# Residual and bias row accumulated in the output's PSUM bank of a sequence mixer, and gathers of the expert choice issued six experts ahead

## The chip, the cores and the metric

The kernel runs on one core of one Trainium2 chip, as a single launch. The metric is the device time of that launch in microseconds (us), the median of several runs. Differences of about 0.3% are what the measurement can tell from no change.

## What is computed

The reference is two transformer blocks over `x[16, 512, 128]` in fp32: causal attention with ALiBi slopes, an expert-choice feed-forward layer (8 experts, each takes the 256 tokens with its highest router score), a gated convolution and state-space mixer, and a top-2-of-8 mixture of experts. The change touches the second and the third. The expert choice, with `xf` the normalised tokens:

```python
G, idx = jax.lax.top_k(softmax(xf @ router_w + router_b).T, K)      # K = 256 tokens for each of 8 experts
toks = xf[idx]
h1 = relu(einsum('ekh,ehf->ekf', toks, w1) + b1[:, None, :])
eo = einsum('ekf,efh->ekh', h1, w2) + b2[:, None, :]
y = zeros_like(xf).at[idx.reshape(-1)].add((eo * G[..., None]).reshape(-1, h))
```

The mixer, with `x` here the layer-normalised input (the caller adds the outer residual):

```python
u, v = split(x @ in_proj_w + in_proj_b)
v_local = dwconv(silu(v), conv_w, conv_b)                # 3 taps along time
h_t = a * h_{t-1} + ssm_b * v_local_t;  y_t = ssm_c * h_t + ssm_d * v_local_t
out = (u * silu(y)) @ out_proj_w + out_proj_b
h = out + x
return (h - mean(h)) * rsqrt(var(h) + 1e-5) * ln_w + ln_b
```

## The kernel before

The kernel runs its stages one after the other, each in a block of its own that ends with all engines meeting: attention, projection, choice of tokens, `expert_choice`, `mixer`, gate and dispatch, `experts`.

**expert_choice.** For each of the 8 experts GpSimd (POOL) issues two gathers of 128 rows by indirect DMA into `xg` (L1142). TensorE turns them (`turn`, L1191), computes router logits, the first matrix (`first`, L1204) and the second (`second`, L1216); ScalarE applies the relu, VectorE the gates and the product with the score into `ctr` (L1288). POOL then adds the two tiles of `ctr` to `x_scr` by two indirect DMAs with an add (the scatters, L1157). A scatter waits until `ctr` of its expert is there (`s_ctr`) and until every earlier scatter has landed (`s_sc`), because two experts can add to one row. POOL's order is written out: gathers of experts 0 to 2; then for each expert e the gathers of e+3 followed by the scatters of e. Weights are loaded by SyncE in two buffers each.

**mixer.** Sixteen sequences of 512 positions. The loop is software-pipelined (`skewed`): in step s each engine works on block s (normalise, turn, input projections), block s-1 (convolution, recurrence, gate) and block s-2 (output projection, residual, second norm). Buffers alternate by the parity of the block. The order of the work on each engine in a step is:

- TensorE (PE): output projection of s-2 into `psO` (L1428, 4 products), turn of s into `psX` (L1435), `psV` (L1440), `psU` (L1443).
- ScalarE (ACT): `xn` of s (L1463, 4 tiles), copy `xT` (L1468), `dv` of s-1, `vs` (L1477) and `c0` (L1479) of s, `ys` of s-1 (L1485), `hn` of s-2 (L1493, 4 tiles).
- VectorE (DVE): tap 0 of s-1 (L1550), `ho` = `psO` + `xo` of s-2 (L1560), tap 2 of s-1 (L1550), 4 `bn_stats` of `ho` (L1566), the seven small instructions of `chain` (L1512 to L1522) that end in `veps`, scan of s-1 (L1579), `y` (L1582), 4 `bn_stats` of s+2 (L1504), `z` of s-1 (L1592).
- POOL: `rstd` (a power, L1384) and `shift` (L1386) from `veps`, `t2` (L1402), `xo` = `xn` + bias row (L1407), `t1` (L1410), a short instruction (L1413), the final sum into `x_all` (L1414).

`chain` serves x of block s+1 and h of block s-2 at once, so `shift` releases `hn` of s-2 and then `xn` of s+1.

Of the kernel before, what the change touches and what calls it, by code (L numbers as in the profile page):

```python
# [13 lines left out]
F32 = mybir.dt.float32  # L14
# [8 lines left out]
P = 128  # L23
# [1078 lines left out]
def expert_choice(nc, idx, tab, rw, rb, w1, b1, w2, b2, xbuf, ident, nb):  # L1102

    nt = nb * TT
    FT = 4
    SCORE = 6
    with ExitStack() as ctx:
        sb = lambda name, shape, dt: ctx.enter_context(nc.sbuf_tensor("ec_" + name, shape, dt))
# [30 lines left out]
        def _(pool):  # L1139
# [4 lines left out]

            for e in range(3):
                gather(e)
            for e in range(E):
                if e + 3 < E:
                    pool.wait_ge(s_xg[e % 3], 32 * (e // 3 + 1))
                    gather(e + 3)  # L1150

                pool.wait_ge(s_ctr, e + 1)
                if e:
                    pool.wait_ge(s_sc, 32 * e)
                for k in (2 * e, 2 * e + 1):
                    off = bass.IndirectOffsetOnAxis(ap=idx[:, k:k + 1], axis=0)
                    pool.indirect_dma_start(xr, off, ctr[:, k, :], None, compute_op=ALU.add).then_inc(s_sc, 16)  # L1157
# [155 lines left out]
def mixer(nc, x_all, xbuf, ident, win, wout, prm, rows, loads, nb):  # L1313

    with ExitStack() as ctx:
# [18 lines left out]
            "a", "b", "c", "minus_mean", "var", "veps", "rstd", "shift"))  # L1334
        xn, xT, vs, c0, vl, hs, dv, ys, z, xo, ho, hn = (two(n, s) for n, s in (
            ("xn", [P, TT, C]), ("xT", [P, T]), ("vs", [P, T + 2]), ("c0", [P, T]), ("vl", [P, T]), ("hs", [P, T]),
            ("dv", [P, T]), ("ys", [P, T]), ("z", [P, T]), ("xo", [P, TT, C]), ("ho", [P, TT, C]), ("hn", [P, TT, C])))
        t1, t2 = sb("t1", [P, TT, C], F32), sb("t2", [P, TT, C], F32)
# [4 lines left out]
        psO = [ps("psO0"), ps("psO1")]  # L1343
        s_w, s_p, s_set, s_xs, s_hs, s_n, s_r, s_xn, s_tr, s_xT, s_uv, s_vs, s_c0, s_c, s_dv, s_y, s_ys, s_z, s_o, s_xo, \
            s_h, s_hn, s_t1, s_x3, s_pre, s_v, s_ahead = (sem(n) for n in (
                "weights", "powers", "set", "x_stats", "h_stats", "chain", "shift", "xn_ready", "turned", "xT_ready", "uv_ready",
                "v_ready", "conv0", "conv", "dv_ready", "y_ready", "silu_y", "z_ready", "out_ready", "xo_ready", "h_ready",
                "hn_ready", "t1_ready", "x3_ready", "prepared", "v_product", "loaded_ahead"))
# [25 lines left out]
        def _(pool):  # L1374
# [15 lines left out]
            def step(s, n):  # L1390
# [10 lines left out]
                if live(b, nb):  # L1401
                    pool.tensor_tensor(t2[:], x_all[:, bass.ds(TT * b, TT), :], rows_s[:, 2], ALU.add)  # L1402
                if live(s, nb):
                    pool.wait_ge(s_xn, s + 1)
                    if not isinstance(s, int) or s >= 2:
                        pool.wait_ge(s_h, s - 1)
                    pool.tensor_tensor(xo[n][:], xn[n][:], rows_s[:, 0], ALU.add).then_inc(s_xo, 1)  # L1407
                if live(b, nb):
# [9 lines left out]
        def _(pe):  # L1418
            pe.wait_ge(s_w, 16 * (TT + 3))

            def step(s, n):
                b = s - 2
                if live(b, nb):
                    pe.wait_ge(s_z, b + 1)
                    if not isinstance(b, int) or b >= 2:
                        pe.wait_ge(s_h, b - 1)
                    for t in range(TT):
                        i = pe.matmul(psO[n][:, P * t:P * t + P], z[n][:, P * t:P * t + P], wout_s[:], start=True, stop=True)  # L1428
                    i.then_inc(s_o, 1)
                if live(s, nb):  # L1430
                    pe.wait_ge(s_xn, s + 1)
# [15 lines left out]
        def _(act):  # L1447
# [7 lines left out]
            def step(s, n):  # L1455
                m = 1 - n
                if live(s, nb):
                    act.wait_ge(s_r, s + 1)
                    if not isinstance(s, int) or s >= 2:
                        act.wait_ge(s_tr, s - 1)  # L1460
                        act.wait_ge(s_xo, s - 1)
                    for t in range(TT):
# [23 lines left out]
                if live(s - 2, nb):  # L1486
# [4 lines left out]
                    for t in range(TT):  # L1491
                        u = TT + t
                        i = act.activation(hn[n][:, t], ho[n][:, t], ACT.Identity, bias=shift[:, u:u + 1], scale=rstd[:, u:u + 1])  # L1493
                    i.then_inc(s_hn, 1)
# [3 lines left out]
        def _(dve):  # L1498
# [36 lines left out]
            dve.wait_ge(s_pre, 4)  # L1535

            def step(s, n):
                m = 1 - n
# [715 lines left out]
```

## Time and profile before

| | us |
|---|---|
| median of 3 runs | 1726.03 (1721.57 to 1727.01) |
| the profiled execution | 1718.55 |
| its span, first to last instruction | 1716.7 |
| expert choice, from the first gather to the last scatter | 875.4 to 948.0 |
| mixer, from its first instruction to its last | 950.3 to 1130.5 |

The span has a tensor clock of 0.836 of full speed on average. The mixer's steady steps lie between 980 and 1126 us. Rows of the timeline give start and duration of one instruction (or of equal neighbours, with their count), and in brackets how long the engine was idle before it and what ended that.

### The profile page before, as it was taken

To read this page: it belongs to the slowest core of one execution; us is meant where nothing else is said; L and a number is where in the kernel's file an instruction comes from. 1 tells how busy PE (TensorE), PEld (TensorE's weight loads), DVE (VectorE), ACT (ScalarE), POOL (GpSimd) and SP (SyncE) were. 2 spreads that over 40 slices of the span, in tenths; PEclk is the share of its full clock that TensorE was granted. 3 is DMA by queue.
4 is the path that set the end of the run, shared out by engine and by line. 5 is a ranking of instruction groups with operands and counts; after the bars stand their busy time and mean duration, and the time that the engine had idled before them with its cause. 6 is when DMAs were issued, how large, how long until landed. Compare 5 with 4: busy or idle time off the path is not lost. (4 is left out here: it accounts for less than half of the span.)

```text
span 1716.7 us, 35014 instructions
## 1 busy us (share of the span) xinstructions
PE 1226.1 (71%) x9530; PEld 728.2 (42%) x9531; DVE 1164.2 (68%) x3272; ACT 837.4 (49%) x2073; POOL 990.9 (58%) x1023
## 2 busy tenths in 40 slices
PE   2788788888777888584046366627099999999997
PEld 1334333433333433373035133327066655555555
DVE  2778687777666778386732499866866666666664
ACT  1567576766666677111212366634144444444443
POOL 1465455655454553241035399965268888888887
PEclk7899899999989999565568655655599999999999
DMA  4433333433322431362023200300423333333333
GB/s 112 144 82 92 73 105 90 96 88 93 77 71 77 95 96 62 116 222 73 0 85 73 68 26 25 118 6 24 181 38 41 42 42 43 41 41 42 41 43 40
DMA packets 88430, 125.49 MB, mean 73 GB/s; under 512 B 22434, under 2 KB 59106, under 8 KB 84242
## 3 DMA queue, kind: packets, MB, share of 16 engines
q0 software_dynamic: 41120, 45.22, 16.7%
q1 hardware_dynamic: 39170, 65.85, 11.5%
q10 hardware_dynamic: 8032, 12.93, 2.1%
q8 instruction: 74, 1.21, 0.3%
q14 instruction: 34, 0.28, 0.1%
HBM read 65.72 MB, written 57.68 MB: 72 GB/s over the span
## 5 line engine op out<-in xcount | busy, mean ns | idle before, releaser
L548 DVE TENSOR_REDUCE mx<-psS 128x2 f32<-128x768 f32 (+3 forms) x384 | 386.3, 1041 | 169.7 <-PE psS L441 169.0
L619 ACT ACTIVATE probs<-psE 128x512 f32<-128x512 f32 (+2 forms) x768 | 345.2, 523 | 162.4 <-PE psE L455 160.3
L344 POOL TENSOR_SCALAR_AFFINE_SELECT probs<-probs 128x512 f32<-128x512 f32 x256 | 162.1, 642 | 261.2 <-ACT probs L619 260.9
L2034 POOL DMA_INDIRECT out<-ex_y,ex_idx x144 | 236.7, 1644 | 47.5 <-issue 43.0
L455 PE MATMUL psE<-qop,kop 63*128 63x512 bf16 (+3 forms) x1024 | 195.5, 312 | 78.9 <-DVE rest L514 34.8
L467 PE MATMUL psY<-probs,vaug 128*32 128x512 f32 (+3 forms) x2048 | 180.8, 464 | 9.7 <-POOL probs L344 9.7
L2025 POOL DMA_INDIRECT ex_xg<-expert_tab,ex_idx x144 | 141.9, 985 | 66.0 <-issue 41.7
L2008 DVE SCALAR_TENSOR_TENSOR ex_h<-ex_psG,ex_w,ex_up 128x352 f32<-128x352 f32 x144 | 84.0, 584 | 106.1 <-PE ex_psG L2075 95.4
L441 PE MATMUL psS<-kop,qop 61*128 61x128 bf16 (+3 forms) x1024 | 141.8, 310 | 0.0
L2092 PE MATMUL ex_psY<-ah_w3s,ex_hT 128*128 (+1 forms) x864 | 133.2, 290 | 0.9 <-ACT ex_hT L2103 0.7
L455 PEld LDWEIGHTS psE<-qop,kop 63*128 63x128 bf16 x1024 | 65.1, 96 | 160.2 <-ACT probs L619 91.5
L436 PE MATMUL psS<-maskq,spread 64*128 64x128 bf16 (+2 forms) x1536 | 115.2, 227 | 19.9 <-DVE mx L548 19.8
L2102 ACT ACTIVATE ex_hT<-ex_psH 128x256 f32<-128x256 f32 x144 | 55.2, 383 | 135.5 <-PE ex_psH L2068 127.3
L2092 PEld LDWEIGHTS ex_psY<-ah_w3s,ex_hT 128*128 128x128 f32 (+1 forms) x864 | 107.6, 191 | 21.1 <-issue 3.5
L2074 PE MATMUL ex_psU<-ah_w1s,ex_xT 128*128 x288 | 110.1, 464 | 0.5 <-ACT ex_xT L2113 0.5
L436 PEld LDWEIGHTS psS<-maskq,spread 64*128 64x128 bf16 x1536 | 57.6, 96 | 122.6 <-DVE mx L548 84.9
L2075 PE MATMUL ex_psG<-ah_w2s,ex_xT 128*128 x288 | 109.3, 461 | 0.0
L467 PEld LDWEIGHTS psY<-probs,vaug 128*32 128x32 f32 x2048 | 69.4, 114 | 63.6 <-issue 31.3
L2113 ACT ACTIVATE ex_xT<-ex_psX 128x128 f32<-128x128 f32 x144 | 39.9, 277 | 107.3 <-PE ex_psX L2061 106.9
L2061 PE MATMUL ex_psX<-ident,ex_xg 128*128 128x128 f32 x144 | 47.6, 331 | 39.6 <-DMA ex_xg<-expert_tab,ex_idx 32.1
L2068 PE MATMUL ex_psH<-ident,ex_h 128*128 128x128 f32 (+1 forms) x432 | 72.2, 275 | 0.2 <-issue 0.2
L2107 ACT ACTIVATE ex_up<-ex_psU 128x352 f32<-128x352 f32 x144 | 66.7, 463 | 7.8 <-PE ex_psU L2074 0.8
(318 smaller groups left out, 2524.6 us busy)
## 6 DMA issues: line engine op xcount, KB each, us to landing
y_scr<-ysb SPq DMA_DIRECT2D x64, 256.0 KB, 3.1
qkv_scr<-parts SPq DMA_DIRECT2D x32, 384.0 KB, 3.2
qop<-qkv_scr POOLq DMA_DIRECT2D x30, 192.0 KB, 4.4
kop<-qkv_scr POOLq DMA_DIRECT2D x30, 192.0 KB, 5.9
expert_tab<-table_rows SPq DMA_DIRECT2D x1, 4352.0 KB, 13.1
pj_num<-y_scr SPq DMA_DIRECT2D x16, 256.0 KB
pj_rec<-rec_scr SPq DMA_DIRECT2D x16, 256.0 KB
x_scr<-x_all ACTq DMA_DIRECT2D x16, 256.0 KB, 3.3
```

Of the source, the lines that this page charges most:

```text
L344: pool.affine_select(diag, diag, [[0, HG], [1, P]], ALU.is_ge, 0.0, base=0, channel_multiplier=-1).then_inc(s_msk, 1)
L436: pe.matmul(out[:, :, P * j + lo:w], spread[rows, lo // HALF], maskq[rows, 0:nh, 0:P - lo], start=(lo == 0), stop=False, skip_group_check= ...
L441: mm = pe.matmul(out[:, h, :], half(qop[n], p, ROW_MAX)[:, hh, P * j:P * j + P], half(kop[n], p, ROW_MAX)[:, hh, 0:w], start=False, stop=( ...
L455: mm = pe.matmul(ring_bank(st, u)[:, W[j] * h:W[j] * h + W[j]], half(kop[m], p, ROW_END)[:, hh, P * j:P * j + P], half(qop[m], p, ROW_END) ...
L467: mm = pe.matmul(psY[32 * h:32 * h + 32, P * k:T], vaug[m_v][:, k, HG * e_v + h, :], probs[e_v % 2][k][:, h, :], start=(k == 0), stop=(k = ...
L548: dve.tensor_reduce(out, src, AX, ALU.max).then_inc(s_su, 1)
L619: act.activation(probs[st % 2][j][:, 2 * p + h0:2 * p + h0 + nh, :].rearrange("p h q -> p (h q)"), ring_bank(st, k)[:, 0:nh * W[j]], ACT.E ...
L2025: pool.indirect_dma_start(xg[t % 4][:], None, ytab, bass.IndirectOffsetOnAxis(ap=idx[t % 8][:], axis=0))\
L2034: pool.indirect_dma_start(out, bass.IndirectOffsetOnAxis(ap=idx[t % 8][:], axis=0), y[m][:], None, compute_op=ALU.add).then_inc(s_sc[m], 16)
L2074: pe.matmul(psU[n][:, 0:DE], xT[n][:], flat(w1s[:, e, :]), start=True, stop=True).then_inc(s_g2, 1)
L2075: pe.matmul(psG[n][:, 0:DE], xT[n][:], flat(w2s[:, e, :]), start=True, stop=True).then_inc(s_g, 1)
L2092: i = pe.matmul(psY[:, 0:C], hT[m][0:wd, f], flat(w3s[0:wd, f, e, :]), start=(f == 0), stop=(f == len(FC) - 1))
```

## The change

In the expert choice, POOL issues the gathers of six experts before the first scatter (each from the fourth on waits until the gather three before it has landed), and then the gathers of expert e+5 ahead of the scatters of expert e.

In the mixer, `xo` and `ho` go. TensorE opens the bank of block r in the step after `psX`, `psV`, `psU` of r: one bf16 product of a matrix of ones with three rows that hold the bias row split in three bf16 parts, then four fp32 products of the identity with `xn`, all accumulating; the output projection is then accumulated on top. `bn_stats` and `hn` read `psO` in place of `ho`. On VectorE `bn_stats` of h now stands ahead of tap 2. Nine VectorE instructions ahead of the first step make the parts of the bias row.

```diff
-            for e in range(3):
-                gather(e)
+            def gather_next(e):
+                if 3 <= e < E:
+                    pool.wait_ge(s_xg[e % 3], 32 * (e // 3))
+                if e < E:
+                    gather(e)
+
+            for e in range(AHEAD):            # AHEAD = 6
+                gather_next(e)
             for e in range(E):
-                if e + 3 < E:
-                    pool.wait_ge(s_xg[e % 3], 32 * (e // 3 + 1))
-                    gather(e + 3)
-
+                if e:
+                    gather_next(e + AHEAD - 1)
                 pool.wait_ge(s_ctr, e + 1)
...
 (POOL, mixer)
-                if live(s, nb):
-                    pool.wait_ge(s_xn, s + 1)
-                    if not isinstance(s, int) or s >= 2:
-                        pool.wait_ge(s_h, s - 1)
-                    pool.tensor_tensor(xo[n][:], xn[n][:], rows_s[:, 0], ALU.add).then_inc(s_xo, 1)
...
 (TensorE)
                     pe.wait_ge(s_z, b + 1)
-                    if not isinstance(b, int) or b >= 2:
-                        pe.wait_ge(s_h, b - 1)
                     for t in range(TT):
-                        i = pe.matmul(psO[n][:, P * t:P * t + P], z[n][:, P * t:P * t + P], wout_s[:], start=True, stop=True)
+                        i = pe.matmul(psO[n][:, P * t:P * t + P], z[n][:, P * t:P * t + P], wout_s[:], start=False, stop=(t == TT - 1),
+                                      skip_group_check=True)
                     i.then_inc(s_o, 1)
+                if live(s - 1, nb):
+                    r = s - 1
+                    if isinstance(r, int) and r == 0:
+                        pe.wait_ge(s_bias, 9)
+                    if not isinstance(r, int) or r >= 2:
+                        pe.wait_ge(s_hn, r - 1)
+                    pe.matmul(psO[1 - n][:], ones[:], bias3[:], start=True, stop=False, skip_group_check=True)
+                    for t in range(TT):
+                        i = pe.matmul(psO[1 - n][:, P * t:P * t + P], ident[:], xn[1 - n][:, t], start=False, stop=False, skip_group_check=True)
+                    i.then_inc(s_open, 1)
...
 (ScalarE)
-                        act.wait_ge(s_xo, s - 1)
+                        act.wait_ge(s_open, s - 1)
...
-                        i = act.activation(hn[n][:, t], ho[n][:, t], ACT.Identity, bias=shift[:, u:u + 1], scale=rstd[:, u:u + 1])
+                        i = act.activation(hn[n][:, t], psO[n][:, P * t:P * t + P], ACT.Identity, bias=shift[:, u:u + 1], scale=rstd[:, u:u + 1])
...
 (VectorE, once)
+            row = rows_s[0:BROWS, 0].rearrange("p t c -> p (t c)")
+            dve.memset(ones[:], 1.0).then_inc(s_bias, 1)
+            dve.memset(bias3[:], 0.0).then_inc(s_bias, 1)
+            dve.tensor_copy(biashi[:], row).then_inc(s_bias, 1)
+            dve.wait_ge(s_bias, 3)
+            dve.tensor_tensor(biasrest[0][:], row, biashi[:], ALU.subtract).then_inc(s_bias, 1)
+            dve.tensor_copy(bias3[0:1], row[0:1]).then_inc(s_bias, 1)
...
 (VectorE, each step)
                 tap(0)
                 if live(s - 2, nb):
-                    b = s - 2
-                    dve.wait_ge(s_o, b + 1)
-                    dve.wait_ge(s_xo, b + 1)
-                    if not isinstance(b, int) or b >= 2:
-                        dve.wait_ge(s_hn, b - 1)
-                    dve.tensor_tensor(ho[n][:], psO[n][:].rearrange("p (t c) -> p t c", t=TT), xo[n][:], ALU.add).then_inc(s_h, 1)
-                tap(2)
-                if live(s - 2, nb):
-                    dve.wait_ge(s_h, s - 1)
+                    dve.wait_ge(s_o, s - 1)
                     dve.memset(carry[:], 0.0)
                     for t in range(TT):
-                        i = dve.bn_stats(stats[:, TT + t], ho[n][:, t])
+                        i = dve.bn_stats(stats[:, TT + t], psO[n][:, P * t:P * t + P])
                     i.then_inc(s_hs, 1)
+                tap(2)
```

## Rows read from the trace of the kernel before

**Rows 1.** Window: width, busy (count) of PE, PEld, DVE, ACT, POOL, clock, DMA, GB/s.

```profile
980.00:1126.00 146.00, 90.20 (x228) 45.83 (x228) 127.47 (x341) 91.44 (x184) 128.31 (x107) 0.59 0.15 51
```

**Rows 2.** Timeline of POOL, expert choice: start, us, engine, line, tiles, idle before.

```profile
884.35 0.94 POOL L1142 DMA_INDIRECT ec_xg<-norm_tab,idx  x1 [0.30 <-issue]
894.78 1.63 POOL L1157 DMA_INDIRECT x_scr<-ec_ctr,idx  x1 [9.49 <-DVE ec_ctr L1288]
...
902.21 1.62 POOL L1157 DMA_INDIRECT x_scr<-ec_ctr,idx  x1 [1.30 <-DMA x_scr<-ec_ctr,idx]
...
911.58 1.62 POOL L1157 DMA_INDIRECT x_scr<-ec_ctr,idx  x1 [3.28 <-DVE ec_ctr L1288]
...
932.75 1.56 POOL L1157 DMA_INDIRECT x_scr<-ec_ctr,idx  x1 [2.49 <-DMA x_scr<-ec_ctr,idx]
...
944.60 1.55 POOL L1157 DMA_INDIRECT x_scr<-ec_ctr,idx  x1 [2.56 <-DMA x_scr<-ec_ctr,idx]
```

**Rows 3.** Groups by line, expert choice: busy, mean ns, idle before and releaser.

```profile
L1191 PE MATMUL ec_psX<-ident,ec_xg 128*128 128x128 f32 x16 | 4.2, 351 | 25.4 <-DMA ec_xg<-norm_tab,idx 25.4
```

**Rows 4.** Timeline of the mixer's first steps, all engines.

```profile
970.11 0.75 DVE L1550 SCALAR_TENSOR_TENSOR mx_c<-mx_vs,mx_prm,mx_c 128x512 f32<-128x512 f32 x1 [5.41 <-ACT mx_c L1479]
...
971.67 0.66 PE L1435 MATMUL mx_psX<-ident,mx_xn 128*128 128x128 f32 x4 [1.46 <-ACT mx_xn L1463]
...
973.01 1.13 PE L1440 MATMUL mx_psV<-mx_xT,mx_win 128*128 128x512 f32 x2 [0.69 <-ACT mx_xT L1468]
```

**Rows 5.** Timeline of one steady step of the mixer, all engines.

```profile
1042.65 0.75 DVE L1592 SCALAR_TENSOR_TENSOR mx_z<-mx_psU,mx_prm,mx_ys 128x512 f32<-128x512 f32 x1
...
1043.45 1.16 PE L1428 MATMUL mx_psO<-mx_wout,mx_z 128*128 128x128 f32 x8 [1.36 <-DVE mx_z L1592]
...
1044.65 0.69 DVE L1560 TENSOR_TENSOR mx_ho<-mx_psO,mx_xo 128x512 f32<-128x512 f32 x1 [0.17 <-PE mx_psO L1428]
1045.26 0.90 DVE L1550 SCALAR_TENSOR_TENSOR mx_vl<-mx_vs,mx_prm,mx_c 128x512 f32<-128x512 f32 x1
...
1046.06 1.11 PE L1435 MATMUL mx_psX<-ident,mx_xn 128*128 128x128 f32 x4 [1.45 <-ACT mx_xn L1463]
1046.09 0.28 DVE L1566 BATCH_NORM_STATS2 mx_stats<-mx_ho 128x6 f32<-128x128 f32 x1
...
1047.51 1.27 POOL L1414 TENSOR_TENSOR x_all<-mx_t 128x512 f32 x1
1047.51 1.29 DVE L1516 SCALAR_TENSOR_TENSOR mx_nrm_c<-mx_nrm_a 128x8 f32<-128x8 f32 x1
...
1047.86 2.07 PE L1440 MATMUL mx_psV<-mx_xT,mx_win 128*128 128x512 f32 x2 [0.69 <-ACT mx_xT L1468]
...
1049.12 0.17 DVE L1522 TENSOR_SCALAR mx_nrm_veps<-mx_nrm_var 128x8 f32<-128x8 f32 x1
...
1049.37 2.58 POOL L1384 TENSOR_TENSOR mx_nrm_rstd<-mx_nrm_veps,mx_mhalf 128x8 f32<-128x8 f32 x1 [0.59 <-DVE mx_nrm_veps L1522]
...
1050.54 0.75 DVE L1582 SCALAR_TENSOR_TENSOR mx_hs<-mx_hs,mx_bc,mx_dv 128x512 f32<-128x512 f32 x1
...
1051.50 0.61 ACT L1485 ACTIVATE mx_ys<-mx_hs 128x512 f32<-128x512 f32 x1
...
1052.20 0.75 DVE L1592 SCALAR_TENSOR_TENSOR mx_z<-mx_psU,mx_prm,mx_ys 128x512 f32<-128x512 f32 x1
1052.26 1.65 ACT L1493 ACTIVATE mx_hn<-mx_ho,mx_nrm_shift,mx_nrm_rstd 128x128 f32<-128x128 f32 x4
...
1053.09 2.07 PE L1428 MATMUL mx_psO<-mx_wout,mx_z 128*128 128x128 f32 x8 [1.45 <-DVE mx_z L1592]
1053.41 1.72 POOL L1407 TENSOR_TENSOR mx_xo<-mx_xn,mx_rows 128x512 f32<-128x512 f32 x1
1053.81 1.64 ACT L1463 ACTIVATE mx_xn<-x_all,mx_nrm_shift,mx_nrm_rstd 128x128 f32 x4
```

**Rows 6.** Groups by line, window 980 to 1123 (15 output projections, 14 of psV).

```profile
L1440 PE MATMUL mx_psV<-mx_xT,mx_win 128*128 128x512 f32 x28 | 29.0, 1141 | 9.6 <-ACT mx_xT L1468 9.6
...
L1428 PE MATMUL mx_psO<-mx_wout,mx_z 128*128 128x128 f32 x120 | 23.8, 359 | 28.2 <-DVE mx_z L1592 28.2
```

More of the change, by code:

```diff
@@ L1106, in expert_choice @@
     SCORE = 6
+    AHEAD = 6
     with ExitStack() as ctx:
@@ L1334, in mixer @@
             "a", "b", "c", "minus_mean", "var", "veps", "rstd", "shift"))
-        xn, xT, vs, c0, vl, hs, dv, ys, z, xo, ho, hn = (two(n, s) for n, s in (
+        xn, xT, vs, c0, vl, hs, dv, ys, z, hn = (two(n, s) for n, s in (
             ("xn", [P, TT, C]), ("xT", [P, T]), ("vs", [P, T + 2]), ("c0", [P, T]), ("vl", [P, T]), ("hs", [P, T]),
-            ("dv", [P, T]), ("ys", [P, T]), ("z", [P, T]), ("xo", [P, TT, C]), ("ho", [P, TT, C]), ("hn", [P, TT, C])))
+            ("dv", [P, T]), ("ys", [P, T]), ("z", [P, T]), ("hn", [P, TT, C])))
+        BROWS = 65
+        bias3, biashi, biasmid = (sb("bias_" + n, [BROWS, T], BF16) for n in ("rows", "hi", "mid"))
+        biasrest = [sb(f"bias_rest{k}", [BROWS, T], F32) for k in range(2)]
+        ones = sb("ones", [BROWS, P], BF16)
         t1, t2 = sb("t1", [P, TT, C], F32), sb("t2", [P, TT, C], F32)
@@ L1343, in mixer @@
         psO = [ps("psO0"), ps("psO1")]
-        s_w, s_p, s_set, s_xs, s_hs, s_n, s_r, s_xn, s_tr, s_xT, s_uv, s_vs, s_c0, s_c, s_dv, s_y, s_ys, s_z, s_o, s_xo, \
-            s_h, s_hn, s_t1, s_x3, s_pre, s_v, s_ahead = (sem(n) for n in (
+        s_w, s_p, s_set, s_xs, s_hs, s_n, s_r, s_xn, s_tr, s_xT, s_uv, s_vs, s_c0, s_c, s_dv, s_y, s_ys, s_z, s_o, s_open, \
+            s_bias, s_hn, s_t1, s_x3, s_pre, s_v, s_ahead = (sem(n) for n in (
                 "weights", "powers", "set", "x_stats", "h_stats", "chain", "shift", "xn_ready", "turned", "xT_ready", "uv_ready",
-                "v_ready", "conv0", "conv", "dv_ready", "y_ready", "silu_y", "z_ready", "out_ready", "xo_ready", "h_ready",
+                "v_ready", "conv0", "conv", "dv_ready", "y_ready", "silu_y", "z_ready", "out_ready", "residual_in_psum", "bias_parts",
                 "hn_ready", "t1_ready", "x3_ready", "prepared", "v_product", "loaded_ahead"))
@@ L1535, in _ @@
             dve.wait_ge(s_pre, 4)
+            row = rows_s[0:BROWS, 0].rearrange("p t c -> p (t c)")
[5 more added lines that the diff above has]
+            dve.tensor_copy(bias3[0:1], row[0:1]).then_inc(s_bias, 1)
+            dve.wait_ge(s_bias, 5)
+            dve.tensor_copy(biasmid[:], biasrest[0][:]).then_inc(s_bias, 1)
+            dve.tensor_copy(bias3[32:33], biasrest[0][32:33]).then_inc(s_bias, 1)
+            dve.wait_ge(s_bias, 7)
+            dve.tensor_tensor(biasrest[1][:], biasrest[0][:], biasmid[:], ALU.subtract).then_inc(s_bias, 1)
+            dve.wait_ge(s_bias, 8)
+            dve.tensor_copy(bias3[64:65], biasrest[1][64:65]).then_inc(s_bias, 1)
             def step(s, n):
```

## The prediction

> **What bounds the kernel now.** I read the windows by stage first, then the timelines of the two stages that the change touches, then the groups of one line. Two places matter, and they add up independently, since each stage ends with all engines meeting.
>
> In the expert choice POOL's timeline shows a chain of eight scatters, each held until the one before has landed [rows 2]. Where nothing stands between two scatters they start 11.85 us apart for two (932.75 to 944.60), 5.93 each. Where gathers stand between, the first interval is 7.43, and the next is 9.37 because `ctr` came last: TensorE had waited for rows gathered behind a scatter. TensorE waits 25.4 us in this stage for gathered rows [rows 3].
>
> In the mixer's steady part VectorE is busy 127.47 of 146 us and POOL 128.31 [rows 1], but neither is simply full. Output projections start at 1043.45 and 1053.09, 9.64 apart [rows 5]. The 143 us of [rows 6] hold fifteen output projections, 9.6 per step with the last two draining; thirteen steps are steady, and I take each at 9.6. Three loops meet in one step [rows 5]:
>
> (A) From `z` to `hn`: `z` starts 1042.65, `psO` 1043.45 and takes 1.16, `ho` 1044.65, tap 2 1045.26, `bn_stats` 1046.09, then `chain`, whose `veps` ends 1049.29, `rstd` 1049.37, `hn` 1052.26: 9.61. Inside it one 8-column instruction of `chain` took 1.29 instead of 0.17, because POOL's 1.27 us sum started at the same 1047.51.
>
> (B) From `hn` back to `z`: `hn` 1052.26, `xn` ends 1055.45 (3.19), `psX` to `ys` 5.44 (1046.06 to 1051.50), `ys` 0.61, `z` 0.1, with a hand-over of 0.05: 9.4. The loop A then B covers two steps, so it asks for (9.61 + 9.4) / 2 = 9.5 per step, and with a slow `psO` (2.07, as at 1053.09) 0.9 more in A: 9.95. It is the bound.
>
> (C) ScalarE with TensorE in one step, without any wait for `shift`: `hn` and `xn` 3.19, hand-over 0.05, `psX` to `ys` 5.44, `ys` 0.6: 9.3. So this loop stands only 0.3 under the step.
>
> The mean granted clock there is 0.59 [rows 1], that is, mostly the 1.2 GHz level. `psV` is always at the lower level (29.0 us over 14, 2.07 each), `psO` at either in about equal parts (23.8 over 15 is 1.59, between 1.16 and 2.07) [rows 5, 6]; at the higher level `psV` took 1.13 and `psX` 0.66 against 1.11 [rows 4, 5]. So the two together give back 0.94 + 0.45 = 1.4 us per step when the clock is up.
>
> **Expert choice, part by part.** Gathers of experts 3 to 5 now precede the first scatter. The last gather of expert 3 ended at 885.3, and POOL then sat idle 9.49 us until 894.78 [rows 2]: four more gathers at 1.25 us pitch (0.94 and 0.30 idle) need 5.0 us of these, plus some wait for expert 2 to land. The first scatter stays at 894.78, the second at 902.21, since it has a pair of gathers before it as now. The third has the last pair before it: 7.43 again, 909.64, and `ctr` of expert 2 is no longer late, as its neighbours' rows are there and TensorE needs not wait. Then five intervals of 5.93: the last scatter starts 939.3 against 944.60. That is -5.3. Bounds: intervals stretched to 7.43 throughout by the weight loads beside them would give 894.78 + 52.0 = 946.8, nothing gained (+2 at worst); -6 if the second pair costs less.
>
> **Mixer, what goes.** `ho` leaves VectorE: 0.61 from its start to the next, in loop A. `xo` leaves POOL: 1.72 [rows 5]. It lies in neither loop, but it moves `t1` and the last sum forward by that much. The sum will then meet tap 2 or the end of `bn_stats` instead of `chain`; the lock of 1.12 may go, or may merely fall on tap 2. I keep both ends, 0 and 1.12, and take half. `bn_stats` moved ahead of tap 2 only reorders loop A. `hn` and `bn_stats` read PSUM: `z` with one PSUM operand takes 0.75 and `y` from SBUF 0.75 [rows 5], so I cost this at nothing.
>
> The Trainium skill's page "VectorE: DVE Perf Modes" (section on the TRN2 errata) gives a fixed 120 cycles for a PSUM source against 58 for SBUF, 65 ns more; four `bn_stats` in each of 16 steps would cost 4.1 us by it. The two equal 0.75 us rows do not show it, and I leave it out of the sum.
>
> **Mixer, what comes.** Per step TensorE gets four fp32 products of the size of `psO`'s: 0.95 us at the higher clock and 1.85 at the lower (the two rows less the drain at the end, about 0.2). The bf16 product of 512 columns has no twin here; half of `psV`, 0.57 or 1.04, bounds it from above and nothing from below; I take 0.25 and 0.45. So opening a bank is 1.2 or 2.3. Its place is between `psO` and `psX`, where TensorE now waits 1.45 for `xn` [rows 5]. It also waits for `hn` of the block before in that bank, which ends 1.65 after `hn` starts, about when `psO` at the higher clock is done; behind it stand `psX`, and behind that ScalarE's `xT`. At the higher clock: `z` start, 0.80, 0.95, 1.2: `psX` could start 2.95 after `z`, and `xn` is ready 3.2 after: hidden. At the lower: 0.80 + 1.85 + 2.3 = 4.95, 1.7 late.
>
> Step lengths that follow (D is the new loop `z`, `psO`, opening, `psX` to `ys`, `z`):
> - clock high throughout: A 9.61 - 0.61 - half of 1.12 = 8.4, B 9.4 - 1.4 = 8.0, C 7.9: 8.2.
> - high in `psO`, low in `psX` and `psV`: C 9.3, A and B 8.9: 9.3.
> - low in `psO` and opening, high after: D 4.95 + 5.44 - 1.4 + 0.7 = 9.7.
> - low throughout: D 4.95 + 5.44 + 0.7 = 11.1.
>
> What mixture? Now the clock is up after the unbroken run of `psV` and `psU` and falls after a stretch that holds `psO` alone. [...] I take most steps at 9.3 to 9.7 with some 8.2 and few 11.1: mean 9.2, -0.4 in thirteen steps, -5.2.
>
> **Ends of the mixer.** The nine preparing instructions (none above 0.75, so between 1 and 6.7 us, say 4) run while VectorE waits 5.41 us for `c0` [rows 4]; `shift` of block 1 slips with them but ScalarE needs it only near 970: nothing, at most +1.4. The two draining steps and the last block lose `ho` in their chain: -0.6 each, -1.4.
>
> **Sum.** -5.3 - 5.2 - 1.4 = -11.9 on a profiled execution of 1718.55 (span 1716.7 and 1.85 around it). The median of the runs, 1726.03, is 7.5 above that execution; I take the difference from the median: 1714. Within 0.3% (5.2 us) I call no change.
>
> **The rivals.**
> 1. *TensorE becomes the bound.* If the clock stays at the lower level, every step is 11.1: +1.5 x 13 = +19.5, with the rest +13: 1739. For it: clock 0.59 and every steady `psV` at 2.07. Against: `psO` at 1.16 in about half of the steps [rows 1, 6]. It decides from a mean step of 10.1 up. Chance 0.10.
> 2. *The added products keep the clock up.* Steps of 8.2: -18, in all -25: 1701. Chance 0.13. The Trainium skill's page "TensorE: Matmul & The Clock Gate" (Part 1) says that the throttled state is the default and activity releases it; a busier TensorE would by that rule go this way. The trace agrees in so far as the clock rises behind `psV` and `psU`.
> 3. *Loop C holds the mixer.* It is 0.3 under the step already; if the clock pattern stays and the openings at low clock cost as much as `ho` gives, the mixer stays at 9.6 and only the ends and the expert choice gain: -6.7, 1719. Chance 0.17.
> 4. *The scatters do not close up*, because the landing behind weight loads stays near 4 us, with the mixer as in 3: 1724 to 1726. Chance 0.08.
>
> My forecast (1706 to 1719) has 0.52.
>
> **Range and chances.** From 1701 to 1726: it takes in rivals 2 to 4 and leaves out rival 1 and a tail below. Faster by over 0.3% (under 1720.8): the forecast, rival 2 and most of 3, 0.76. Within 0.3%: the rest of 3 and rival 4, 0.15. Slower: 0.09.
>
> **What would show it.** Right: `xg` gathers of six experts without a scatter between, the last scatter 5 us sooner after the first, TensorE's 25.4 us of waiting mostly gone; in the mixer, `psO` openings that end before `xn` where the clock is high, no 1.29 us row in `chain`, a mean clock of 0.65 to 0.8, steps of 9.2. Wrong: `psX` late behind the opening in most steps, `bn_stats` well over 0.28, scatters over 6 us apart with nothing between, or the preparation of the bias rows delaying the first tap.

## The result and the profile after

| | before | after |
|---|---|---|
| median of 4 runs each, us | 1723.8 (1719.12 to 1727.01) | 1702.09 (1695.05 to 1705.22) |
| ratio | | 0.987, 95% interval 0.9828 to 0.9913 |
| profiled execution, us | 1718.55 | 1705.22 |
| its span, us | 1716.7 | 1703.0 |

The change makes the kernel faster, by 21.7 us in the medians. The same kernel run again (six runs against eleven) gave 1702.78 against 1720.59, 17.8 us and 0.9901 (0.988 to 0.9922); the two intervals overlap, and I take the gain as 17 to 22 us.

The two profiled executions differ by 13.7 us in their spans. Cut at the instructions that begin and end each stage, the difference lies here:

| stretch, us | before | after | difference |
|---|---|---|---|
| start to the first gather (not touched) | 875.40 | 878.06 | +2.66 |
| first gather to the mixer's first POOL instruction | 74.86 | 69.86 | -5.0 |
| from there to the first `psO` | 26.88 | 26.56 | -0.3 |
| 15 intervals between `psO` starts | 142.56 | 132.14 | -10.4 |
| of these, the 13 steady ones | 124.58 | 116.42 | -8.2 |
| last `psO` to the gate stage | 13.72 | 12.96 | -0.8 |
| rest (not touched) | 583.28 | 583.42 | +0.1 |

So the touched stages give 16.5 us, and 2.7 of them are hidden in the profiled pair by the untouched first half.

**Expert choice.** POOL's timeline after, to be held against [rows 2] (columns as there):

```profile
892.01 0.95 POOL L1143 DMA_INDIRECT ec_xg<-norm_tab,idx  x1 [0.30 <-issue]
897.75 1.63 POOL L1162 DMA_INDIRECT x_scr<-ec_ctr,idx  x1 [4.79 <-DVE ec_ctr L1293]
...
905.19 1.61 POOL L1162 DMA_INDIRECT x_scr<-ec_ctr,idx  x1 [1.30 <-DMA x_scr<-ec_ctr,idx]
...
911.60 1.64 POOL L1162 DMA_INDIRECT x_scr<-ec_ctr,idx  x1 [0.30 <-issue]
...
917.91 1.56 POOL L1162 DMA_INDIRECT x_scr<-ec_ctr,idx  x1 [2.77 <-DMA x_scr<-ec_ctr,idx]
...
942.38 1.56 POOL L1162 DMA_INDIRECT x_scr<-ec_ctr,idx  x1 [2.53 <-DMA x_scr<-ec_ctr,idx]
```

The four extra gathers end where POOL stood idle before: of the 9.49 us ahead of the first scatter 4.79 are left, and that scatter comes 19.69 us after the first gather (before 19.38). No scatter waits for `ctr` any more but the first. The eight lie 44.63 us apart from first to last, where they lay 49.82 apart. TensorE's wait for gathered rows fell from 25.4 us [rows 3] to 15.1, and what is left is the arrival of the first rows:

```profile
L1196 PE MATMUL ec_psX<-ident,ec_xg 128*128 128x128 f32 x16 | 3.7, 321 | 15.1 <-DMA ec_xg<-norm_tab,idx 15.1
```

**Mixer.** The windows of the kernel after (columns as in [rows 1]; the second stretch is used for every kernel below, and in those whose mixer ends sooner up to 11 us at its end hold draining steps):

```profile
980.00:1126.00 146.00, 82.48 (x350) 56.06 (x350) 116.89 (x345) 94.56 (x189) 107.67 (x99) 0.79 0.16 53
985.00:1095.00 110.00, 74.06 (x302) 49.56 (x303) 95.84 (x267) 76.24 (x158) 86.02 (x74) 0.83 0.20 65
```

In the second stretch the kernel before had a granted clock of 0.61. The intervals between output projections are now 7.52, 8.23, 9.23, 8.32, 9.23, 9.70, 8.32, 9.24, 9.65, 8.32, 9.23, 9.57, 8.23, 9.15, 8.20: three kinds of step. Here is one of the short kind, from the timeline of PE, VectorE and POOL:

```profile
1025.91 0.75 DVE L1614 SCALAR_TENSOR_TENSOR mx_z<-mx_psU,mx_prm,mx_ys 128x512 f32<-128x512 f32 x1 [1.32 <-PE mx_psU L1457]
1026.58 0.74 DVE L1579 SCALAR_TENSOR_TENSOR mx_c<-mx_vs,mx_prm,mx_c 128x512 f32<-128x512 f32 x1
...
1026.71 1.16 PE L1430 MATMUL mx_psO<-mx_wout,mx_z 128*128 128x128 f32 x8 [1.40 <-DVE mx_z L1614]
...
1027.71 0.38 PE L1440 MATMUL mx_psO<-mx_bias_rows,mx_ones 65*128 65x512 bf16 x1
...
1027.92 0.29 DVE L1587 BATCH_NORM_STATS2 mx_stats<-mx_psO 128x6 f32<-128x128 f32 x1 [0.60 <-issue]
1027.93 1.05 PE L1442 MATMUL mx_psO<-mx_xn,ident 128*128 128x128 f32 x8
...
1028.72 0.73 DVE L1579 SCALAR_TENSOR_TENSOR mx_vl<-mx_vs,mx_prm,mx_c 128x512 f32<-128x512 f32 x1
1028.79 1.80 POOL L1418 TENSOR_TENSOR x_all<-mx_t 128x512 f32 x1
...
1028.87 0.65 PE L1449 MATMUL mx_psX<-ident,mx_xn 128*128 128x128 f32 x4
1029.38 1.24 DVE L1526 TENSOR_TENSOR mx_nrm_a<-mx_stats 128x8 f32<-128x8 f32 x1
```

And the next step, whose `psO` is in part and whose opening is wholly at the lower clock:

```profile
1034.23 0.75 DVE L1614 SCALAR_TENSOR_TENSOR mx_z<-mx_psU,mx_prm,mx_ys 128x512 f32<-128x512 f32 x1
...
1035.03 1.77 PE L1430 MATMUL mx_psO<-mx_wout,mx_z 128*128 128x128 f32 x8 [2.84 <-DVE mx_z L1614]
...
1036.60 0.63 PE L1440 MATMUL mx_psO<-mx_bias_rows,mx_ones 65*128 65x512 bf16 x1
...
1037.03 1.91 PE L1442 MATMUL mx_psO<-mx_xn,ident 128*128 128x128 f32 x8
...
1038.73 0.64 PE L1449 MATMUL mx_psX<-ident,mx_xn 128*128 128x128 f32 x4
...
1043.46 0.75 DVE L1614 SCALAR_TENSOR_TENSOR mx_z<-mx_psU,mx_prm,mx_ys 128x512 f32<-128x512 f32 x1 [0.30 <-issue]
```

There are four things to see here. Opening the bank takes 1.16 us at the higher clock (1027.71 to 1028.87) and 2.13 at the lower (1036.60 to 1038.73). Behind it `psX` starts at once; in the second step `z` to `psX` is 4.50, and the step is 9.23. The short step is 8.32. And the lock did not go: POOL's final sum, now begun at 1028.79, holds the next VectorE instruction with two inputs, `nrm_a`, which takes 1.24 us where such an instruction takes 0.16; before it was `nrm_c` with 1.29 [rows 5]. In three of the thirteen steady steps it is tap 2 that is held (1.66 to 1.81 us).

VectorE's round from `z` to `z` shows where the short step's time went. Before it was 9.55 (1042.65 to 1052.20), of which VectorE waited 0.17 for `psO` [rows 5]; now it is 8.32, of which it waits 0.60. `ho` is -0.61; tap 0 is -0.43 (0.74 for 1.17); tap 2 is -0.17; the short gaps around both groups of `bn_stats` and in `chain` are -0.45; the added wait for `psO` is +0.43: -1.23. So the shorter tap 0 gave nothing by itself: from `z` until `psO` is there it is 2.0 us in both. These are the places where the time went, not yet the cause; for that see below, where POOL's round is read.

The groups of the same stretch (busy, mean ns, idle before):

```profile
L1507 ACT ACTIVATE mx_hn<-mx_psO,mx_nrm_shift,mx_nrm_rstd 128x128 f32<-128x128 f32 x48 | 18.0, 454 | 1.6 <-POOL mx_nrm_shift L1395 1.6
L1454 PE MATMUL mx_psV<-mx_xT,mx_win 128*128 128x512 f32 x26 | 17.5, 759 | 8.9 <-ACT mx_xT L1482 8.9
...
L1579 DVE SCALAR_TENSOR_TENSOR mx_vl<-mx_vs,mx_prm,mx_c 128x512 f32<-128x512 f32 x12 | 11.9, 992 | 0.0
L1526 DVE TENSOR_TENSOR mx_nrm_a<-mx_stats 128x8 f32<-128x8 f32 (+1 forms) x13 | 10.7, 823 | 0.0
L1587 DVE BATCH_NORM_STATS2 mx_stats<-mx_psO 128x6 f32<-128x128 f32 x48 | 10.6, 284 | 6.2 <-issue 6.2
```

### The profile page after: what moved, and what is told of

The parts are those of the page before. It is cut to its first block and busy times, and to the rows that moved or that the text cites. A ratio compares the mean times of both kernels' runs of the same rounds, so it can differ in the third digit from the quotient of the medians.

```text
span 1703.0 us, 35233 instructions
## 1 busy us (share of the span) xinstructions
PE 1222.3 (72%) x9672; PEld 744.5 (44%) x9675; DVE 1156.8 (68%) x3265; ACT 834.9 (49%) x2073; POOL 966.1 (57%) x1007
```

## The experiments

Theory: VectorE's own round is the bound before, so taking `ho` out of it pays, and the clock pays only after that. Rival: the loop A then B is the bound, and a higher clock alone shortens it. A third possibility, that POOL's round is the bound and `xo` the part that mattered, got no kernel of its own; every kernel here has both `ho` and `xo` or neither. The traces of two of them speak for it, as shown below. All results, each against the kernel before on the same chip (three groups, whose medians of before the first row gives), with the mean of the thirteen steady steps and the granted clock between 985 and 1095 us:

| kernel | median us | ratio, 95% interval | mean step | clock |
|---|---|---|---|---|
| before | 1718.5 to 1720.6 | | 9.58 | 0.61 |
| choice only | 1709.98 | 0.9965 (0.9937 to 0.9993) | 9.61 | 0.59 |
| mixer only | 1702.01 | 0.9906 (0.9874 to 0.9937) | 8.76 | 0.88 |
| opening in a spare bank | 1711.88 | 0.9957 (0.9937 to 0.9977) | 9.55 | 0.81 |
| no opening, no residual | 1702.37 | 0.9911 (0.9877 to 0.9946) | 9.03 | 0.59 |
| tap 2 first | 1696.02 | 0.9853 (0.9824 to 0.9883) | 8.79 | 0.83 |
| opening behind `psU` | 1699.03 | 0.9877 (0.985 to 0.9905) | 8.80 | 0.83 |
| no final sum | 1692.13 | 0.9846 (0.9823 to 0.9869) | 8.57 | 0.82 |
| eight experts ahead | 1699.14 | 0.9891 (0.9867 to 0.9915) | 8.69 | 0.90 |
| the new kernel again | 1702.78 | 0.9901 (0.988 to 0.9922) | 8.90 | 0.86 |
| filler product | 1697.9 | 0.9881 (0.9857 to 0.9906) | 8.73 | 0.89 |
| tap 2 first, filler | 1697.18 | 0.9871 (0.9844 to 0.9898) | 8.55 | 0.93 |
| tap 2 first, opening behind `psU` | 1698.86 | 0.9883 (0.9858 to 0.9909) | 8.60 | 0.88 |

Four of these profiles hold the same mixer as the new kernel (mixer only, eight ahead, again, and the result's own): 8.76, 8.69, 8.90, 8.96. So one profile tells a mean step to about 0.27 us, and smaller differences are not read. The four stand in the order of their clocks (0.88, 0.90, 0.86, 0.83), the highest clock with the shortest step. "No final sum" and "no opening, no residual" leave a part of the result out.

### The halves by themselves

The new expert choice with the old mixer (all edits of the mixer undone, one of them shown), and the old expert choice with the new mixer:

```diff
 (choice only)
-                        i = dve.bn_stats(stats[:, TT + t], psO[n][:, P * t:P * t + P])
+                        i = dve.bn_stats(stats[:, TT + t], ho[n][:, t])
...
 (mixer only)
-            for e in range(AHEAD):
-                gather_next(e)
+            for e in range(3):
+                gather(e)
```

> The gathers of the new kernel with the mixer of before. Theory (the two parts add up, each stage by itself): the expert choice, from the first gather to the mixer's first instruction, 69.9 us as in the new kernel instead of 74.9, the mixer as before (output projections 9.6 us apart), so about -5 us, ratio 0.997. Rival (the timed difference of 21.7 us holds something that the profiles do not show, and it sits in the expert choice): -10 us or more.

> The mixer of the new kernel with the gathers of before. Theory: 15 intervals between the first and the last output projection in 132 us instead of 142.6, in all -11.5 us, ratio 0.993; the expert choice 74.9 us. Rival (the timed difference holds something more, and it sits with the mixer): -17 us or more.

Choice only: 0.9965, and 71.37 us from the first gather to the mixer for 74.86. Mixer only: 0.9906 and a mean step of 8.76. The new order gave 69.1 to 71.4 us in all eleven profiles with six experts ahead, the old one 74.86 and 74.94. The two parts add up, within their intervals, to the whole; the mixer carries about two thirds of it (16.5 us of 25.0 by the medians, 11.5 of 16.5 by the stages). Both medians gained more than the stages of their profiles had led to expect, 8.5 us for 5 and 16.5 for 11.5, and lie between the theory and its rival. The new kernel's second timing, -17.8 us, agrees with the 16.5 of the stages.

### The clock without the lighter VectorE and POOL, and the reverse

The first kernel keeps `ho` and `xo` and gives TensorE the same products, into a bank that nobody reads. The second drops `ho`, `xo` and the opening: it leaves the residual and the bias row out of the mixer's output.

```diff
 (opening in a spare bank, against choice only)
+                if live(s - 1, nb):
...
+                    pe.matmul(psD[:], ones[:], bias3[:], start=True, stop=False, skip_group_check=True)
+                    for t in range(TT):
+                        i = pe.matmul(psD[:, P * t:P * t + P], ident[:], xn[1 - n][:, t], start=False, stop=False, skip_group_check=True)
...
 (no opening, no residual, against the kernel after)
-                    pe.matmul(psO[1 - n][:], ones[:], bias3[:], start=True, stop=False, skip_group_check=True)
-                    for t in range(TT):
-                        i = pe.matmul(psO[1 - n][:, P * t:P * t + P], ident[:], xn[1 - n][:, t], start=False, stop=False, skip_group_check=True)
-                    i.then_inc(s_open, 1)
```

> The new gathers, and the mixer of before with the products that open a bank added at their place but written to a spare bank that nobody reads; xo and ho stay, so TensorE has the new work and VectorE and GpSimd the old. Theory 1 (most of the mixer's gain comes from TensorE's clock, which the added products keep up): granted clock about 0.8 in the steady steps, psV mostly at 1.13 us, steps of 8.9 to 9.3 us instead of 9.6. Theory 2 (the gain comes from ho and xo going): steps of 9.6 us or more, since loop A still holds ho and the openings come on top.

> The new gathers, and the new mixer without the products that open a bank: the output projection starts its own group, so residual and bias are left out of the mixer's result. VectorE and GpSimd have the new work, TensorE the old. Theory 1 (clock): the clock falls back to about 0.6, psV at 2.07 us, and ScalarE's loop with TensorE (C, 9.3) holds the step: 9.3 us. Theory 2 (ho and xo): steps of 9.0 us or less, as in the new kernel, or shorter, since nothing stands between psO and psX.

The steady window of the kernel before and of these two, in this order:

```profile
985.00:1095.00 110.00, 71.98 (x187) 37.02 (x188) 99.60 (x261) 74.23 (x151) 99.92 (x81) 0.61 0.20 68
```

```profile
985.00:1095.00 110.00, 72.54 (x292) 48.63 (x292) 100.16 (x258) 75.04 (x153) 99.68 (x81) 0.81 0.20 65
```

```profile
985.00:1095.00 110.00, 73.30 (x188) 37.97 (x188) 84.61 (x254) 74.06 (x155) 82.52 (x76) 0.59 0.18 63
```

With the products in the spare bank the clock rises from 0.61 to 0.81. Its group of `psV`, and below it that of the kernel without an opening:

```profile
L1460 PE MATMUL mx_psV<-mx_xT,mx_win 128*128 128x512 f32 x22 | 15.2, 780 | 7.5 <-ACT mx_xT L1488 7.5
```

```profile
L1444 PE MATMUL mx_psV<-mx_xT,mx_win 128*128 128x512 f32 x22 | 21.9, 1095 | 7.6 <-ACT mx_xT L1471 7.6
```

So `psV` is mostly at its short length, the loop A then B is 1.4 us shorter over two steps in all those, and the step should be 8.8 by it. It is 9.55. VectorE's timeline in that kernel:

```profile
1015.08 0.75 DVE L1627 SCALAR_TENSOR_TENSOR mx_z<-mx_psU,mx_prm,mx_ys 128x512 f32<-128x512 f32 x1
...
1017.26 0.69 DVE L1595 TENSOR_TENSOR mx_ho<-mx_psO,mx_xo 128x512 f32<-128x512 f32 x1 [0.23 <-PE mx_psO L1438]
...
1020.07 1.28 DVE L1536 SCALAR_TENSOR_TENSOR mx_nrm_c<-mx_nrm_a 128x8 f32<-128x8 f32 x1
...
1024.60 0.75 DVE L1627 SCALAR_TENSOR_TENSOR mx_z<-mx_psU,mx_prm,mx_ys 128x512 f32<-128x512 f32 x1
```

From `z` to `z` 9.52 us, of which VectorE waits 0.23 for `psO`. That looks full, but 1.28 of it is `nrm_c`, a 0.17 us instruction held by POOL's sum: a hold is a wait for POOL. And VectorE's rounds are not all like this one. In the kernel before, the five steady rounds with a `psO` of 2.07 have VectorE without an instruction for 1.2 to 1.5 us, and they last 9.62 to 9.79; the five in the middle of the stretch with 0.4 to 0.7 without one last 9.52 to 9.68. A bound that leaves a whole us of slack in five of thirteen rounds is not the bound.

POOL has no such slack. Here is its timeline before, in a round in which VectorE waited 1.29 for a `psO` of 2.07; the sum of 1047.51, the `rstd` of 1049.37 and the `xo` of 1053.41 belong to it and stand in [rows 5]:

```profile
1052.02 0.20 POOL L1386 TENSOR_TENSOR mx_nrm_shift<-mx_nrm_minus_mean,mx_nrm_rstd 128x8 f32<-128x8 f32 x1
1052.19 1.26 POOL L1402 TENSOR_TENSOR mx_t<-x_all,mx_rows 128x512 f32<-128x512 f32 x1
...
1055.10 1.26 POOL L1410 TENSOR_TENSOR mx_t<-mx_hn,mx_rows 128x512 f32<-128x512 f32 x1
1056.43 0.53 POOL L1413 TENSOR_TENSOR mx_waited<-mx_mhalf 128x1 f32<-128x1 f32 x1
1056.92 1.26 POOL L1414 TENSOR_TENSOR x_all<-mx_t 128x512 f32 x1
1059.14 2.58 POOL L1384 TENSOR_TENSOR mx_nrm_rstd<-mx_nrm_veps,mx_mhalf 128x8 f32<-128x8 f32 x1 [0.96 <-DVE mx_nrm_veps L1522]
```

Its waits between 985 and 1095 us, before, with the opening in a spare bank, and in the new kernel (two lines):

```profile
POOL mx_nrm_rstd L1384 <- DVE mx_nrm_veps L1522: 8.4, 11, 1.0
```

```profile
POOL mx_nrm_rstd L1394 <- DVE mx_nrm_veps L1542: 9.5, 12, 1.1
```

```profile
POOL mx_nrm_rstd L1393 <- DVE mx_nrm_veps L1536: 14.2, 13, 1.6
POOL mx_t L1414 <- ACT mx_hn L1507: 7.9, 12, 1.3
```

Before, POOL waits for `veps` alone, and `veps` waits in turn for POOL: in every steady step an instruction of `chain` (`nrm_c`, `nrm_a` or `minus_mean`) is held until 0.02 to 0.03 us after POOL's sum has ended, and `veps` follows 0.6 to 1.0 us behind. So the loop closes on POOL: sum, the rest of `chain`, `rstd`, `shift`, `t2`, `xo`, `t1`, sum. `xo` is in it with 1.72 us (1.26 to 1.27 in the steps where tap 0 does not run beside it, so a part is a hold by VectorE). `ho` is not in it, and no product of TensorE is. That is why the clock did nothing: ten rounds of `rstd` take 96.35 us before (991.86 to 1088.21) and 96.34 with the spare bank (983.49 to 1079.83), at clocks of 0.61 and 0.81, although one interval of `psO` is 10.88 there and the one behind it 8.68. In the new kernel ten rounds take 89.40, and POOL waits for `hn` as well: its round is no longer the bound.

Without `ho`, `xo` and the opening, at a clock of 0.59, the step is 9.03. Against 9.58, then: the clock alone -0.03, the work taken from VectorE and POOL alone -0.55, all together -0.62 to -0.89. The timed medians say the same: 1709.98 for choice only, 1711.88 with the spare bank, 1702.37 without `ho`, `xo` and opening. So the rival falls, and a higher clock is worth nothing as long as POOL's round stands. Behind the shortened rounds, opening and clock together stand 0.07 to 0.34 under the kernel with neither, which is about the spread of one profile, and their timed ratios (0.9901 and 0.9911) can't be told apart. That `xo` was the part that mattered rather than `ho` is read from these traces; no run takes one of them away alone.

### Where the lock falls

The first kernel puts tap 2 back ahead of `bn_stats`; the second leaves out POOL's final sum, so that the mixer's result does not get into `x_all`.

```diff
 (tap 2 first)
                 tap(0)
+                tap(2)
...
-                tap(2)
...
 (no final sum)
-                    pool.tensor_tensor(waited[:], mhalf[:, 0:1], mhalf[:, 0:1], ALU.add)
-                    pool.tensor_tensor(x_all[:, bass.ds(TT * b, TT), :], t1[:], t2[:], ALU.add).then_inc(s_x3, 1)
+                    pool.tensor_tensor(waited[:], mhalf[:, 0:1], mhalf[:, 0:1], ALU.add).then_inc(s_x3, 1)
```

> The new kernel with tap 2 put back ahead of the four bn_stats of h, so that VectorE works on it while TensorE makes the output projection. Theory (VectorE's own round from z to z is what a step waits for, and 0.6 us of it is the wait for psO in front of bn_stats): steps 0.4 to 0.6 us shorter where the clock is high (7.8 instead of 8.3), 5 to 7 us in all against the new kernel. Rival (the openings behind a slow psO, or ScalarE's loop, hold the step): under 2 us.

> The new kernel without GpSimd's last instruction of each step: the sum of t1 and t2 isn't written, so the mixer's result is left out of x. Theory (that instruction holds VectorE up for about 1.1 us in the chain or in tap 2): the row of 1.23 us at the head of the chain falls to about 0.2 and steps where the clock is high fall from 8.3 to about 7.5. Rival (the lock lies beside the round that decides): the row falls, the steps don't.

The group of tap 2 with tap 2 first, and then tap 2 and `nrm_a` without the final sum:

```profile
L1579 DVE SCALAR_TENSOR_TENSOR mx_vl<-mx_vs,mx_prm,mx_c 128x512 f32<-128x512 f32 x13 | 22.2, 1705 | 0.7
```

```profile
L1578 DVE SCALAR_TENSOR_TENSOR mx_vl<-mx_vs,mx_prm,mx_c 128x512 f32<-128x512 f32 x12 | 8.8, 734 | 0.0
...
L1525 DVE TENSOR_TENSOR mx_nrm_a<-mx_stats 128x8 f32<-128x8 f32 (+1 forms) x13 | 2.1, 163 | 0.1
```

In the new kernel tap 2 has a mean of 992 and `nrm_a` of 823. With tap 2 first the lock moves from `nrm_a` (366) to tap 2 (1705), and the short steps fall only from 8.32 to 8.1, where 7.8 was expected. Without the sum both have their plain lengths. The short step is then 7.70 instead of 8.32, so the lock costs 0.6 us of a short step. It is not earned back in the others: without the sum the intervals are 7.7 and 9.1 to 9.7 in turn, mean 8.57, because the next loop takes over there.

### Moving the opening, and holding the clock up

The opening behind `psU`; a product that nobody reads behind `psU` (into a spare bank); and each of them with tap 2 first.

```diff
 (opening behind psU: the block moves)
                     pe.matmul(psU[n][:], win_s[:, 0:C], xT[n][:], start=True, stop=True).then_inc(s_uv, 1)
+                if live(s - 1, nb):
...
+                    pe.matmul(psO[1 - n][:], ones[:], bias3[:], start=True, stop=False, skip_group_check=True)
...
 (filler product)
                     pe.matmul(psU[n][:], win_s[:, 0:C], xT[n][:], start=True, stop=True).then_inc(s_uv, 1)
+                    pe.matmul(psD[:], win_s[:, 0:C], xT[n][:], start=True, stop=True)
```

> The new kernel with the opening of the next bank moved from between psO and psX to behind psU in the same step, where TensorE waits for z in any case. Theory (in the steps of 9.2 to 9.7 us psX starts late behind an opening at the lower clock): psX no longer late, those steps 8.3 to 9, 3 to 7 us in all against the new kernel. Rival (VectorE's round holds these steps as well): no change within 2 us; a loss if the opening at the lower clock now delays psO.

> The new kernel with psU's two instructions issued a second time into a spare bank that nobody reads, in TensorE's wait for z. Theory (steps differ by TensorE's clock alone: 8.3 us where it is high, 9.2 to 9.7 where it is low somewhere): the clock holds for most steps, granted clock over 0.95, mean step 8.3 to 8.5. Rival (the filler itself is in the way, at the lower clock above all, and VectorE's round is unchanged): steps of 8.9 us or more.

> Tap 2 ahead of bn_stats together with the filler products. Theory (the two gains are of different kinds, VectorE's wait for psO and TensorE's clock, and add up): mean step 8.0 to 8.2, some 10 us under the new kernel. Rival (VectorE's lock by GpSimd and ScalarE's loop take over): no better than the filler alone.

> The opening behind psU and tap 2 ahead of bn_stats, without filler. Theory: the gains of both, mean step 8.5 to 8.7. Rival (each only changes which steps fall to the lower clock): 8.8 as for either alone.

With tap 2 first and the filler the clock is nearly full:

```profile
985.00:1095.00 110.00, 74.27 (x331) 45.86 (x331) 101.33 (x270) 77.29 (x158) 88.85 (x78) 0.93 0.18 63
```

In the thirteen steady steps every `psO` takes 1.16 and all but one `psV` 1.13, and ten of them last 8.54 to 8.62, with VectorE busy 101.33 of 110 us (95.84 in the new kernel). In these ten VectorE is without an instruction for 0.28 us only, but its busy time holds two instructions that POOL holds up, tap 0 at 1.29 and tap 2 at 1.64 to 1.71 for 0.74. So even with the clock up the steps do not get under 8.5. The opening behind `psU` gave 8.80, with tap 2 first 8.60 (8.5 to 8.7 expected), the filler alone 8.73. Two theories missed: the filler was to give 8.3 to 8.5 at a clock over 0.95 and has 0.89, and the filler with tap 2 first was to give 8.0 to 8.2 and gave 8.55. The timed ratios of all four, 0.9871 to 0.9883, overlap with the new kernel's 0.9901 and 0.987; so does that of tap 2 first, 0.9853, by a hair. No version with the full result was shown to beat the new kernel.

### All gathers ahead

```diff
-    AHEAD = 6
+    AHEAD = 8
```

> The new kernel with the gathers of all eight experts issued ahead of the first scatter. Theory (a pair of gathers between two scatters makes that interval longer, 7.4 against 5.9 us): first scatter about 0.5 us later, since POOL issues 20 us of gathers, the first two intervals near 6: the expert choice 1.5 to 2 us shorter than in the new kernel. Rival (the early intervals are long because weight loads run beside the scatters): no change.

> The new kernel unchanged, as a reference for the other three and for the size of the whole effect. Theory (the stages of the profiles hold the whole effect, and the first difference of 21.7 us was widened by the spread of few runs): -15 to -18 us, ratio 0.990 to 0.991. Rival (a part of the gain lies outside the two stages): -20 us or more, ratio 0.987.

The scatters close up further, 43.17 us from first to last instead of 44.63, and the first two intervals are 6.31 and 6.79, but the stage is longer, 72.8 us, where 1.5 to 2 us less were expected. First gather and first scatter on POOL:

```profile
870.42 1.11 POOL L1143 DMA_INDIRECT ec_xg<-norm_tab,idx  x1 [88.67 <-POOLq L896]
...
894.44 1.63 POOL L1162 DMA_INDIRECT x_scr<-ec_ctr,idx  x1 [4.14 <-DVE ec_ctr L1293]
```

They lie 24.02 us apart, for 19.69 with six ahead. VectorE's first instruction for the first and for the second expert, with the product of TensorE that the second one reads:

```profile
880.92 0.17 DVE L1268 TENSOR_TENSOR ec_lg<-ec_psX,ec_rbs 128x16 f32<-128x16 f32 x1 [11.81 <-issue]
...
884.65 0.56 PE L1203 MATMUL ec_psX<-ec_rws,ec_xgT 128*128 128x8 f32 x4
...
891.43 0.17 DVE L1268 TENSOR_TENSOR ec_lg<-ec_psX,ec_rbs 128x16 f32<-128x16 f32 x1 [9.08 <-remote]
```

The first expert comes 10.50 us after the first gather, as with six ahead (10.61). The second comes at 21.01, for 14.72 with six ahead, and 6.2 us after TensorE had finished what it reads; by then POOL's last gather had ended (890.30). What VectorE waited for in these 9.08 us the profile does not name, and it stays open. The timed ratio, 0.9891, can't be told from the 0.9901 of the new kernel.

## Why the prediction was right, and where it was not

**Direction and range: right.** 1702.09 lies in 1701 to 1726, near its lower end; the gain of 17 to 22 us is more than the -11.9 of the sum. The direction was argued from a bound that was not the bound (below), so a part of this is luck.

**Expert choice, -5.3: right.** Measured -5.0. The interval with the first pair of gathers is 7.44 as taken; the one with the second only 6.41, with POOL idle no more than 0.30 in front of that scatter; the third and fourth interval take 6.31 and 6.61 and not 5.93; the last three are 5.98, 5.93 and 5.95. The errors cancel: 44.63 against the 44.5 forecast. Rival 4 did not come.

**The cost of opening a bank: right.** 1.2 and 2.3 were taken, 1.16 and 2.13 measured. At the lower clock `z` to `psX` took 4.50 (4.95 forecast; its `psO` was 1.77 and not 2.07), and the 5.44 less 1.4 plus 0.7 that follow were 4.73. So loop D is what the 9.23 steps are made of.

**Step lengths by clock: right within 0.6.** 8.2 forecast for a step with a high clock, 8.23 to 8.32 measured (five of thirteen); 9.7 for low `psO` and opening with the rest high, 9.15 to 9.24 measured (five); 9.3 for a high `psO` with the others low, 9.57 to 9.70 measured (three). So each kind came, but with the last two in reverse order. None was low throughout, so rival 1 did not come.

**The steady mixer, -5.2: the term that was mis-sized.** It measured -8.2, a mean step of 8.96 for the 9.2 forecast (8.69 to 8.96 over four profiles). "I take most steps at 9.3 to 9.7 with some 8.2 and few 11.1" is the step that missed: five of thirteen were at 8.3. No row of the kernel before gives this mixture, it was a choice; the new kernel has five steps of 8.2 to 8.3, five of 9.2 and three of 9.6 to 9.7.

**"It is the bound": wrong.** The loop A then B was said to bind before, and VectorE, "busy 127.47 of 146 us", to be "not simply full". The opening in a spare bank took 1.4 us out of B in most steps, and the step stayed at 9.55. POOL's round was in the rows and was not added up: its sum ends at 1048.78, it waits 0.59 for a `veps` that this sum had held up, and `xo` follows with 1.72 [rows 5]; in the whole steady stretch it waits for nothing else. "It lies in neither loop" priced `xo` at nothing but a shift of the lock, while the traces put it into the loop that was closed. The forecast of the short step, 8.2 for 8.3, came out right by luck: half of its -1.3 was the clock's 1.4 us in B, which gives nothing by itself, and the loss of `xo` was not counted.

**The lock, half of 1.12: about right in size, wrong in picture.** It was to go or to fall on tap 2. In the steps at high clock it stays in `chain`, on an earlier instruction; it fell on tap 2 in three of the thirteen steps. What did shrink is the hold of tap 0 (mean 1201 to 1017 ns).

**Statistics from PSUM at nothing: right.** `bn_stats` takes 284 ns from PSUM, 274 before from `ho`. That is 10 ns and not the 65 of the Trainium skill's page "VectorE: DVE Perf Modes", section on the TRN2 errata, so the measurement decides: 0.6 us in all and not the 4.1 that were estimated from the page. `hn` on ScalarE became shorter, 454 ns for 482.

**Rival 2, the clock kept up: half right.** The granted clock rose to 0.83 (0.61 before), and 1702.09 is next to the rival's 1701. But its steps of 8.2 throughout came in five of thirteen, and the others were 9.15 to 9.70. The rise is caused by the added products: they alone gave 0.81, and without them it is 0.59. This agrees with the Trainium skill's page "TensorE: Matmul & The Clock Gate" (Part 1), by which activity releases the clock. It was not the cause of most of the gain: with `ho` and `xo` in place it gave nothing.

**Rival 3, loop C holds: not seen.** With the clock at 0.59 and no opening the step is 9.03, under the 9.3 of C. Part of that is `hn`, four times 35 ns shorter there (447); the rest I did not trace.

**The ends, -1.4: too small.** -0.3 at the start, -1.39 in the first interval, -0.87 in the last, -0.8 behind it: -3.3. The forecast had counted the draining end only (and three times its 0.6 is 1.8, not 1.4); the filling end gained as much. The preparation of the bias rows, 959.92 to 963.77 or 3.85 us, was hidden as said: the first tap still waited 1.87 us for `c0`, of 5.41 before [rows 4].

## What to carry to other kernels

Before naming a cross-engine loop as the bound, add up each engine's own round and look at what it waits for. The engine to look for is the one whose only wait is for something that its own last instruction held up; a loop over two steps that comes out equal to the step proves nothing. Time in which another engine holds an instruction is not work but a wait for that engine, so the busy share of the one that is held says too much. Work moved from such engines to one that waits pays even where it makes that one busier, and the clock that rises with it showed nothing while the old round stood. When a lock between VectorE and POOL is to be removed, moving its victim moves it to the next instruction of two inputs; here only leaving the holder out removed it.

## What was not expected of the hardware

- POOL's sum of 128x512 takes 1.27 us, or 1.80 when VectorE's tap 2 has begun just before it (1028.72 and 1028.79). An eight-column VectorE instruction that the sum holds takes 1.24 to 1.29 instead of 0.16, and it is the next one with two inputs in SBUF, not `bn_stats`, that is held. The Trainium skill's page "SBUF — State Buffer" (section "SBUF: two separate sides") describes this as an exclusive lock that whichever of the two starts first has for the whole instruction; the traces agree.
- Such holds closed a loop over two engines: in the kernel before, an instruction of VectorE's `chain` ended 0.02 to 0.03 us after POOL's sum in every steady step, and ten rounds took 96.35 and 96.34 us at two different clocks of TensorE.
- Some 1.2 to 2.1 us of added products per step, where TensorE had waited, raised the granted clock of a stretch from 0.61 to 0.81 and brought one `psV` instruction from a mean of 1141 ns [rows 6] to 780, with no change in the step.
- ScalarE reads a 128x128 tile from PSUM 28 ns faster than from SBUF (454 against 482), VectorE's `bn_stats` 10 ns slower.
- With all sixteen gathers queued ahead, VectorE's first work for the second expert came 21.01 us after the first gather instead of 14.72, 6.2 us behind the product that it reads, with an unnamed releaser.
